# A graph kernel's fourth edge pass: the rows of the last sixteen tiles fetched one by one by SyncE instead of gathered by GpSimd

## What is computed

```python
mf = (x @ W_f.T)[row] * ew[:, None]
y_forward = segment_sum(mf, col, num_segments=n_nodes)
mb = (x @ W_b.T)[col] * ew[:, None]
y_backward = segment_sum(mb, row, num_segments=n_nodes)
y = concatenate([y_forward, y_backward], axis=-1) + bias_param
```

## Time and profile before

| | |
|---|---|
| runs | 6908.73 us median of 3 (6907.74 to 6912.01) |
| the profiled execution: span | 6924.5 us (no other time of it is given) |
| GpSimd busy | 4263.7 us, 62% |
| TensorE matmuls busy | 4938.2 us, 71% |
| VectorE busy | 4004.9 us, 58% |
| ScalarE busy | 2213.2 us, 32% |
| granted clock of TensorE, mean; in the fourth and fifth pass | 0.76; 0.50 |
| DMA queues: GpSimd's (software), SyncE's (hardware) | 182592 packets, 463.57 MB; 109036 packets, 113.52 MB |

### The profile page before, as it was taken

The page is one execution under the profiler, slowest core; times in us unless marked ns, Lnnn a source line. Parts: engine busy times, 40 slices in busy tenths (PEclk is TensorE's granted clock), DMA queues, the critical chain, the costliest instruction groups (busy, mean ns, idle before and its releaser), DMA issues. The chain is left out here.

```text
span 6924.5 us, 111617 instructions
## 1 busy us (share of the span) xinstructions
PE 4938.2 (71%) x21780; PEld 3389.1 (49%) x21781; DVE 4004.9 (58%) x9278; ACT 2213.2 (32%) x4089; POOL 4263.7 (62%) x4428
## 2 busy tenths in 40 slices
PE   4566656689999998998888887995555554555553
PEld 3433333357777765675555555553333333333332
DVE  8767667547777775986777776663332222332224
ACT  3433333348888872024333333541000000000000
POOL 1377777727777773004777776005777777777774
PEclk9577777799999998669999999995555555555555
DMA  3133333343333330333333335112221113212112
GB/s 100 43 106 106 106 104 104 105 115 103 103 103 104 103 104 19 120 127 118 105 105 105 105 105 123 42 32 59 66 66 53 53 52 51 52 52 53 52 53 70
DMA packets 291770, 578.41 MB, mean 84 GB/s; under 512 B 86103, under 2 KB 160163, under 8 KB 291501
## 3 DMA queue, kind: packets, MB, share of 16 engines
q0 software_dynamic: 182592, 463.57, 24.8%
q1 hardware_dynamic: 109036, 113.52, 5.3%
HBM read 533.27 MB, written 49.91 MB: 84 GB/s over the span
## 5 line engine op out<-in xcount | busy, mean ns | idle before, releaser
L635 POOL DMA_INDIRECT big<-h_table,stage_i x880 | 855.5, 972 | 381.9 <-PE bank L1037 191.4
L653 POOL DMA_INDIRECT big<-fwd_table,stage_i x880 | 832.5, 946 | 331.2 <-issue 269.3
L683 POOL DMA_INDIRECT big<-x_and_degree,stage_i x888 | 843.9, 950 | 274.8 <-issue 188.5
L998 PE MATMUL bank<-big,oh 128*128 128x257 f32 x1776 | 693.8, 533 | 442.7 <-DVE acc L2022 428.2
L777 POOL DMA_INDIRECT big<-bwd_table,stage_i x832 | 788.2, 947 | 260.1 <-issue 253.1
L1391 ACT ACTIVATE big<-big 128x889 f16<-128x889 f16 x840 | 873.8, 1041 | 200.7 <-PE bank L1048 160.5
L939 PE MATMUL bank<-big,oh 128*128 128x128 f32 x1760 | 455.6, 440 | 563.2 <-DMA big<-fwd_table,stage_i 562.1
L1970 DVE TENSOR_TENSOR acc<-bank,acc 128x1024 f32 x220 | 269.6, 1225 | 936.2 <-PE bank L939 498.1
L1048 PE MATMUL bank<-big 128*128 128x445 f16 (+1 forms) x3360 | 773.1, 352 | 0.0
L998 PEld LDWEIGHTS bank<-big,oh 128*128 128x128 f32 x1776 | 395.7, 252 | 740.7 <-DVE acc L2022 667.8
L970 PE MATMUL bank<-big,oh 128*128 x1760 | 450.8, 438 | 421.6 <-SPq L554 416.5
(11 more groups left out here) (464 smaller groups left out, 7983.3 us busy)
## 6 DMA issues: line engine op xcount, KB each, us to landing
acc<-places_in_block SPq DMA_DIRECT2D x74, 384.0 KB, 3.5
big<-x_and_degree,stage_i POOLq DMA_INDIRECT x888, 2.8
big<-h_table,stage_i POOLq DMA_INDIRECT x880
big<-fwd_table,stage_i POOLq DMA_INDIRECT x880
big<-bwd_table,stage_i POOLq DMA_INDIRECT x832
h_table<-hq SPq DMA_DIRECT2D x50, 128.0 KB, 1.7
x_table<-big SPq DMA_DIRECT2D x25, 256.0 KB, 2.2
x_turned<-turned SPq DMA_DIRECT2D x25, 256.0 KB, 2.0
```

Source lines behind the costliest of these rows:

```text
L635: pool.indirect_dma_start(out=gbuf[:, u % RING, 0:width], out_offset=None, in_=table, in_offset=bass.IndirectOffsetOnAxis(ap=stage_i[:, v, ...
L653: pool.indirect_dma_start(out=last_rows[:, u, :], out_offset=None, in_=table, in_offset=bass.IndirectOffsetOnAxis(ap=stage_i[:, v, u % RIN ...
L683: pool.indirect_dma_start(out=first_bufs[v][:, r, 0:D + 1], out_offset=None, in_=xd_dram, in_offset=bass.IndirectOffsetOnAxis(ap=stage_i[: ...
L998: pe.matmul(bank[u % 4][:, 0:D + 1], oh[:, r, :], first_bufs[v][:, r, 0:D + 1], start=True, stop=True).then_inc(S["mm"], 1)
```

## The change

Three edits, in one diff:

- GpSimd gathers only the 36 full turns of the fourth pass, 864 tiles. The rows of the last 16 tiles, 2048 of them, are fetched by SyncE with one DMA each of 512 bytes, from row numbers in registers. For this the 16 columns of row numbers are copied by GpSimd when they are computed, and stored by SyncE in a small table in DRAM (`rest_dram`), from which SyncE loads 16 at a time into registers. The rows go to two places that are free in the pass: `rest_sets`, behind the 24 tiles of `last_rows`, and `turned`. TensorE waits once per fetched octet (`rest_in`), not per group.
- The loads of own rows move from SyncE's queue to ScalarE's, each pair ahead of the staging of an octet.
- ScalarE stages two octets less, and stages the fifth pass's first octets when octets 105, 106 and 107 are multiplied. The counts of waits follow (`packed_before`, `STAGED`).

```diff
+    rest_dram = nc.dram_tensor("rows_of_last_tiles", [REST, P], I32).ap()
...
-        packed_before = lambda r: by_groups(1, r) if r < GROUPS else THIRD_BASE
+        packed_before = lambda r: by_groups(1, r) - GROUP * 16 * (r < REST_GROUPS) if r < GROUPS else THIRD_BASE
...
+        rest_sets = ring[:, SPAN * P:(SPAN + RING) * P]
...
+        rest_rows_i = stage_r[:, :, :, :].rearrange("p a r w -> p (a r w)")[:, 0:REST].bitcast(I32)
...
-        STAGED = [0] + [OCTETS - WIDE + OCT * k for k in range(4)]
+        STAGED = [0] + [OCTETS - WIDE + OCT * k - (REST // RING if k == 3 else 0) for k in range(4)]
+        rest_in = ((S["gru_in"], 96 + 16 * P * RING), (S["w5_in"], 48 + 16 * P * RING))
...
+            sp.wait_ge(S["s_ready"], 1)
+            sp.dma_start(rest_dram.rearrange("t p -> p t"), rest_rows_i, allow_slow_non_contiguous=True).then_inc(S["x_in"], 16)
             sp.wait_ge(S["slot_w_ready"], 2)
...
-            with sp.Fori(0, NBE) as n:
-                sp.wait_ge(S["f_out"], n + 2)
-                sp.dma_start(hq[:, 0, 0:P], dense_rows(fwd_dram, n)).then_inc(pair["fin_in"][0], 16)
-                sp.dma_start(hq[:, 0, P:D], dense_rows(bwd_dram, n)).then_inc(pair["fin_in"][0], 16)
+            sp.wait_ge(S["x_in"], 48 + 16)
+            row_regs = [sp.alloc_register(f"sp_row{j}") for j in range(16)]
+
+            def fetch_rows(t, rows, landed):
+
+                for p in range(P):
+                    if p % 16 == 0:
+                        sp.load(row_regs, rest_dram[ds(t, 1), p:p + 16])
+                    row = sp.snap(row_regs[p % 16], min_val=0, max_val=NBE * P - 1)
+                    sp.dma_start(rows(p), fwd_dram[ds(row, 1), :]).then_inc(landed, 16)
+
+            with sp.Fori(0, RING) as t:
+                fetch_rows(t, lambda p: rest_sets[p:p + 1, ds(t * P, P)], S["gru_in"])
+            with sp.Fori(0, RING) as t:
+                fetch_rows(t + RING, lambda p: turned[p:p + 1, :, :].rearrange("p a n -> p (a n)")[:, ds(t * P, P)], S["w5_in"])
...
-                some(FULL_TURNS, REST)
...
+            link(pool.tensor_copy(rest_rows_i, s_idx[:, FULL_TURNS * SPAN:TILES]))
...
-                            pe.wait_ge(gd[r], i * (GROUP * 16) + by_groups(k - 3, r) + GROUP * 16)
+                            if not fetched:
+                                pe.wait_ge(gd[r], i * (GROUP * 16) + by_groups(k - 3, r) + GROUP * 16)
+                            elif u == 0:
+                                pe.wait_ge(*rest_in[v])
...
+                        rows = last_rows[:, v * RING + u, :] if not fetched else rest_sets[:, u * P:(u + 1) * P] if v == 0 else \
+                            turned[:, :, :].rearrange("p a n -> p (a n)")[:, u * P:(u + 1) * P]
...
-            def stage_pass(index, k):
-
-                with act.Fori(0, FULL_TURNS - 1) as i:
-                    for v in range(3):
-                        stage_again(i * 3 + v + 3, v, index, k)
-                for octet in range(FULL_TURNS * 3, OCT):
-                    stage_again(octet, octet % 3, index, k)
-
-            stage_pass(s_idx, 2)
+            def own_block(n):
+
+                act.wait_ge(S["f_out"], n + 2)
+                act.dma_start(hq[:, 0, 0:P], dense_rows(fwd_dram, n)).then_inc(pair["fin_in"][0], 16)
+                act.dma_start(hq[:, 0, P:D], dense_rows(bwd_dram, n)).then_inc(pair["fin_in"][0], 16)
+
+            def stage_turn(i, own):
+
+                for v in range(3):
+                    if v < own:
+                        own_block(i * 3 + v)
+                    stage_again(i * 3 + v + 3, v, s_idx, 2)
...
+            with act.Fori(0, NBE // 3) as i:
+                stage_turn(i, 3)
+            stage_turn(NBE // 3, NBE % 3)
+            with act.Fori(NBE // 3 + 1, FULL_TURNS - 1) as i:
+                stage_turn(i, 0)
             for v in range(3):
-                act.wait_ge(S["mm"], (OCT - (OCT - 1 - v) % 3) * RING + before_pass(2) + 8)
+                act.wait_ge(S["mm"], ((FULL_TURNS - 1) * 3 + v + 1) * RING + before_pass(2) + 8)
                 stage(d_idx, v * RING, v)
```

More of the change, by code:

```diff
@@ L348, in build @@
         landed_before = lambda k, r: THIRD_BASE + (GROUP * 16 * (FULL_TURNS + (r < REST_GROUPS)) if r < GROUPS else 0) + 16 * OCT * (k - 3)
-        STAGED = [0] + [OCTETS - WIDE + OCT * k for k in range(4)]
+        STAGED = [0] + [OCTETS - WIDE + OCT * k - (REST // RING if k == 3 else 0) for k in range(4)]
+        rest_in = ((S["gru_in"], 96 + 16 * P * RING), (S["w5_in"], 48 + 16 * P * RING))
+        assert (SPAN + RING) * P <= 2 * RING * (D + 1) and REST == 2 * RING
         blocks_in, blocks_out = ([sem(f"blocks_{n}{q}") for q in range(2)] for n in ("in", "out"))
@@ L920, in scatter_pass, with octet @@
             def scatter_pass(k, kk, slots, shift):
-                def octet(i, v):
+                def octet(i, v, fetched=False):
                     o = i * 3 + v
@@ L936, in octet @@
                             r = 2 * v + u // GROUP
-                            pe.wait_ge(gd[r], i * (GROUP * 16) + by_groups(k - 3, r) + GROUP * 16)
+                            if not fetched:
+                                pe.wait_ge(gd[r], i * (GROUP * 16) + by_groups(k - 3, r) + GROUP * 16)
+                            elif u == 0:
+                                pe.wait_ge(*rest_in[v])
                         b = pe.snap(regs[u], min_val=0, max_val=RING - 1)
-                        mm = pe.matmul(sums[:, ds(b, 1), :].rearrange("p b f -> p (b f)"), oh[:, place, :], last_rows[:, v * RING + u, :],
+                        rows = last_rows[:, v * RING + u, :] if not fetched else rest_sets[:, u * P:(u + 1) * P] if v == 0 else \
+                            turned[:, :, :].rearrange("p a n -> p (a n)")[:, u * P:(u + 1) * P]
+                        mm = pe.matmul(sums[:, ds(b, 1), :].rearrange("p b f -> p (b f)"), oh[:, place, :], rows,
                                        start=False, stop=True, skip_group_check=True)
@@ L947, in scatter_pass @@
                 for v in range(REST // RING):
-                    octet(FULL_TURNS, v)
+                    octet(FULL_TURNS, v, True)
             def packed_pass(slots, shift):
@@ L1575, in _ @@
             staggered(act, PAIRS, 5, state_functions)
-            def stage_pass(index, k):
-                with act.Fori(0, FULL_TURNS - 1) as i:
-                    for v in range(3):
-                        stage_again(i * 3 + v + 3, v, index, k)
-                for octet in range(FULL_TURNS * 3, OCT):
-                    stage_again(octet, octet % 3, index, k)
-            stage_pass(s_idx, 2)
+            def own_block(n):
[7 more added lines that the diff above has]
+                    stage_again(i * 3 + v + 3, v, s_idx, 2)
+            for q in range(2):
+                act.wait_ge(pair["tab_out"][q], BASE["tab_out"] + 48 * PAIRS)
+            with act.Fori(0, NBE // 3) as i:
[3 more added lines that the diff above has]
+                stage_turn(i, 0)
             for v in range(3):
-                act.wait_ge(S["mm"], (OCT - (OCT - 1 - v) % 3) * RING + before_pass(2) + 8)
+                act.wait_ge(S["mm"], ((FULL_TURNS - 1) * 3 + v + 1) * RING + before_pass(2) + 8)
                 stage(d_idx, v * RING, v)
```

## The result

The changed kernel takes **7899.75 us** (median of 4 runs, 7893.02 to 7907.31) against 6910.37 for the kernel before (4 runs, 6907.74 to 6914.18): ratio **1.143**, 95% interval 1.1415 to 1.1447, 989 us more. The forecast was 6993, with a range up to 7200. The profiled execution has a span of 7905.5 us.

What follows compares the result with a forecast made beforehand. GpSimd's gathers were taken to set the pace; after the change SyncE's stream, 942 + 218 + 43 = 1203 us, would be late, moving the thirteenth gather 84.7 us: 6908.7 + 84.7 = 6993 us, range 6886 to 7200.

Steps and rivals of the forecast that it cites:

- Which way, and where: SyncE late, TensorE waiting at octet 109, the fifth pass's thirteenth gather 84.7 us later; slower by over 0.2%: chance 0.64.
- work less 1118.3: Lateness at the change from fourth to fifth pass: SyncE's work in us minus 1118.3, where gain and lateness cancel.
- The DMA, 0.252 us: SyncE's issue of one 512-byte row as one contiguous run: 0.252 us, bounds 0.25 and 0.338.
- The register work and the gaps: SyncE, per row: fused instruction 60 ns, move 29, three gaps of 0.04 us; with the DMA 0.46 us, x 2048 = 942.
- The loads of numbers, 1.7 us: SyncE's 128 loads of 16 registers from DRAM: 1.5 us plus 0.2 for address and gaps, 218 us; bounds 102 and 410.
- The jumps: SyncE's two loops of 128 spelled-out rows: fourteen jumps x 3.1 = 43 us, priced from VectorE's longest loop.
- The gain of 21.7 us: Sixteen gathers fewer on GpSimd and no staging waits: thirteenth gather at 5812.3 instead of 5834.00, if SyncE is in time.
- The own rows on ScalarE at nothing: 100 own-row DMAs of about 0.34 us moved to ScalarE cost nothing, lying beside the gathers; may hold SyncE up a little.
- rival 1: SyncE is in time, its work at or below 1096.6 us; kernel 6887 us; chance 0.30.
- rival 2: It comes out even: SyncE's work between 1105 and 1132 us, gain and lateness cancelling; 6909 us; chance 0.06.
- Rival 3: SyncE's DMA queue sets the pace, a one-row DMA leaving only every 1.0 us; + 930, 7838 us; chance 0.04.
- The range: Kernel time 6886 to 7200 us; upper end from 0.53 a row, 2.2 a load and the jumps, 1410 us of work.

Runs made afterwards that it cites:

- e12: Changed kernel with one fetch loop's row transfers written in seven forms, every eighth row not fetched; 7449.97 us (single run).
- e4: Changed kernel with row numbers loaded to registers from SBUF, put there by one DMA per octet, instead of from DRAM; 7581.95 us (single run).
- e3: Changed kernel with each row's DMA moving 127 of 128 features, so that it stays one run; 7207.18 us (single run).
- e8: As e7, but with loop bodies of 64 rows in place of 128; 7777.7 us, ratio 1.1251 to the kernel before.
- e1: Changed kernel without SyncE's fetch of the 2048 rows and TensorE's wait for them; 6888.24 us, ratio 0.9967 to the kernel before.
- e2: Kernel before with only the loads of own rows moved to ScalarE's queue; 6912.34 us, ratio 1.0001.
- e10: Changed kernel with 127 numbers a row, row numbers from SBUF and loop bodies of 64 rows; 6913.47 us, ratio 0.9998 to the kernel before.
- e7: Changed kernel with row numbers from SBUF and each row written as two halves of 64 numbers landing 512 apart; 7812.94 us, ratio 1.13 to the kernel before.
- e5: Changed kernel fetching only the last octet (1024 rows) by SyncE, GpSimd gathering 872 tiles; 6900.41 us, ratio 0.9981 to the kernel before.
- e9: As e5, with the padding positions' row numbers spread over 128 rows instead of row 0; 6886.66 us, ratio 0.996 to the kernel before.

## Why the prediction was wrong, point by point

- **Which way, and where**: right. SyncE is late, TensorE waits at octet 109 and nowhere else, GpSimd's thirteenth gather waits for it, and the fifth pass keeps its pace. The step "work less 1118.3" also held: 2112 - 1118.3 = 993.7, and counted from the start of SyncE's part the gather comes 6816.47 - 4698.6 - 1124.4 = 993.5 us later.
- **The DMA, 0.252 us**: this is the step that failed. It was 0.553 on average, 616 of the 909 us by which the sum fell short. I priced a row like the four loads of the earlier trace rows, as one contiguous run. They have one run (of 410 and 409 numbers); a row of 128 numbers is cut into 16, as is one of 64 (e12), and one of 127 is not. That a number divides by 16 isn't all that decides, as the 1024 numbers of e4 stay whole; all that were cut had an address in a register. What decides it stays open. The upper bound, 0.338 from the earlier trace rows, fell too: I took 128 rows to be the dearest case, and a single partition with several runs is dearer than 128 partitions. The Trainium skill, "DMA: Bandwidth & Descriptors" (Why a DMA increments its semaphore by 16 and not by 1), says that software can split a contiguous `[1, N]` into an outer dimension that is a multiple of 16, or of the largest factor of N up to 16, so that it is spread over the DMA engines. The packets agree with it for 128 numbers (32 a row) and for 127 (2 a row in e3). What the split costs the issuing engine is read from e3 and e12.
- **The register work and the gaps**: the fused instruction 82 ns instead of 60, the move 29 as said, the three gaps 0.13 together instead of 0.12. A row came to 0.793 us: 2048 x 0.793 = 1625 against 942.
- **The loads of numbers, 1.7 us**: 3.5 each, 451 us against 218, above the upper bound of 3.2. I hadn't thought of the pointer: from DRAM there are two loads in a row, 1.27 and 1.89. The prediction's quoted floor for a register load, about 600 ns (the Trainium skill, "DMA: Bandwidth & Descriptors", Latency and other measured facts), is no floor here: TensorE's load of one register takes 0.305. SyncE's loads of sixteen are all above it, at 0.975 to 1.37 from SBUF.
- **The jumps**: 14 x 2.6 = 36 us against 43. The row of VectorE was a fair analog. e8 shows that a body of half the length doesn't pay it, e12 that length isn't the whole rule.
- **The gain of 21.7 us**: 23.8 measured alone (e1). The own rows on ScalarE at nothing: 0 (e2). That their descriptors may hold SyncE up a little isn't borne out: a row's DMA has the same median beside them and after them.
- **The rivals**: no run that fetches all 2048 rows brought the work below the 1096.6 of rival 1; e10, at 1114.5, shows the crossing, which is rival 2. Rival 3's 7838 lies nearest to the result, but for another reason. Its queue would show as a DMA that is short at first and then stands; here the least is 547 ns, the median 552, the first 697. And the same number of DMAs goes out at 0.234 in e3.
- **The range**: its upper end, 7200, was not the sum of the stated bounds. It kept the DMA at 0.252 and a load at 2.2 us. With the bounds, 0.62 a row and 3.2 a load, the sum is 1270 + 410 + 43 = 1723 us, and the time 7513, still 387 short, since these bounds were themselves taken from other shapes of DMA. 0.14 was left above the range.

## What to carry to other kernels

Many small DMAs were priced here by their issue on the queue's engine, and that price hung on the shape as the instruction carries it, not on the bytes. So look for a row of the same access pattern (the packets per DMA of the queue tell into how many pieces it is cut), and where there is none, put the bound well above the dearest other shape. Count every instruction that the language makes out of one line: a register load from DRAM was two. And when a helper queue has a fixed deadline, give it what it can do in time, even if that is half: here one octet in place of two turns 14% slower into 0.2% faster.

## What the runs showed of the hardware that I had not expected

- On SyncE a DMA of one partition with one run takes 0.234 us to issue, two runs in two partitions 0.248, but two, four or sixteen runs in one partition 0.62, 0.63 and 0.55.
- A load of sixteen registers from DRAM takes 1.27 + 1.89 us on SyncE, the first part for the address; from SBUF 0.975 (e4), in other kernels of the same code up to 1.37 (e7). What makes that difference stays open.
- A row of 128 or 64 numbers, whose address in SBUF is in a register, goes out in 16 pieces; one of 127 goes in one piece, and so do 1024 numbers between fixed addresses (e4).
- A loop body of 402 to 419 instructions jumps back at 2.4 to 3.4 us and fetches its instructions again, one of half the length at 0.2 to 0.3 without fetching. Of two loops of 339 (e12) one does the first and one the second.
- Gathers whose 128 numbers are all the same row land later: groups of four such tiles come every 6.7 us (e5), and every 5.0 when the numbers are spread over 128 rows (e9).
